# GpSimd's order of work inside an attention slot, in a fused cross-attention and coupled feed-forward kernel

## The reference

```
xn  = layernorm(x)                                   # no weights: (x - mean) / sqrt(var + eps)
u   = heads(xn) . heads(ctx) * scale / 4             # 16 heads of 16
a   = softmax(where(mask, -inf, tanh(u) * exp(log_C)))
x   = x + (a . heads(ctx)) @ W_out.T
f   = layernorm(x);  gf = global_net(mean of f over the tokens)
for 3 cycles:
    tf = coupling_net(f)         # 256 -> 256 -> 128 -> 64 -> 1, gelu between, sigmoid at the end
    f  = f + (0.1 + range * (0.7*gf + 0.3*tf - 0.5) * 2) * twist(f)
x   = x + f
```

## Time and profile before

| what | value |
|---|---|
| median of three runs | 1072.22 us (1072.2 to 1073.6) |
| the profiled execution's own time | 1072.12 us |
| its span in the profile | 1070.2 us |
| mean granted TensorE clock | 0.983 of full |
| busy: PE, ACT, DVE, POOL | 977.3, 901.5, 843.8, 573.9 us (91%, 84%, 79%, 54%) |

### The profile page before, as it was taken

The page is one execution under the profiler, slowest core; times in us unless marked ns, Lnnn a source line. Parts: engine busy times, 40 slices in busy tenths (PEclk is TensorE's granted clock), DMA queues, the critical chain, the costliest instruction groups (busy, mean ns, idle before and its releaser), DMA issues.

```text
span 1070.2 us, 21910 instructions
## 1 busy us (share of the span) xinstructions
PE 977.3 (91%) x7260; PEld 526.2 (49%) x7260; DVE 843.8 (79%) x1770; ACT 901.5 (84%) x1121; POOL 573.9 (54%) x1053
## 2 busy tenths in 40 slices
PE   6899999999899999999999999999989999996993
PEld 4456435554355544555445543555435554454431
DVE  3888796997879886987869879699796988688485
ACT  3999778997799978998789977899779997895575
POOL 3366604876068740887228870487606874087204
PEclk7999999999999999999999999999999999999897
DMA  5433002430033200432005310153002430020002
GB/s 118 88 59 58 6 2 44 103 88 1 1 75 89 71 1 1 98 89 48 1 1 118 88 30 1 36 112 88 0 2 69 92 74 1 2 54 31 11 1 80
DMA packets 191119, 51.71 MB, mean 48 GB/s; under 512 B 165920, under 2 KB 174624, under 8 KB 191008
## 3 DMA queue, kind: packets, MB, share of 16 engines
q1 hardware_dynamic: 191008, 50.31, 22.2%
HBM read 33.37 MB, written 16.78 MB: 47 GB/s over the span
## 4 chain that ended last, share of the span: by engine, by line
PE 43%; DVE 16%; POOL 14%; ACT 13%; issue 10%; SPq 2%; DMA 1%; DVEq 0%; POOLq 0%; ACTq 0%
PE ps L1255 8%; PE ps L1269 7%; PE ps L1239 6%; PE ps L1159 5%; ACT probs L914 5%; PE ps L1190 4%; ACT probs L920 3%; PE ps L1175 3%; POOL f_hat L470 3%; PE ps L1278 2%; POOL twisted L525 2%; DVE move_u L780 2%; DVE move_u L801 2%; DVE move_v L782 2%; POOL q_hat L449 2%
## 5 line engine op out<-in xcount | busy, mean ns | idle before, releaser
L914 ACT ACTIVATE probs<-ps,u_scale 120x2048 f32<-120x2048 f32 x128 | 253.7, 1982 | 23.2 <-PE ps L1159 23.2
L920 ACT ACTIVATE probs<-probs,exp_bias,clip 120x2048 f32<-120x2048 f32 x128 | 270.2, 2111 | 0.1
L1269 PE MATMUL ps<-h,w 128*128 128x512 f32 x384 | 185.5, 605 | 14.5 <-ACT h L948 13.8
L1159 PE MATMUL ps<-q_t,k_t 32*120 32x256 f32 x2048 | 148.9, 405 | 21.5 <-ACT probs L914 20.6
L489 POOL TENSOR_TENSOR c<-tok_c 128x16 f32<-128x16 f32 x8 | 1.8, 223 | 277.8 <-issue 277.8
L1190 PE MATMUL ps<-wo_t,of_t 128*128 128x256 f32 x512 | 143.5, 403 | 1.0 <-DVE xy L717 1.0
L692 DVE STREAM_TRANSPOSE o_t<-ps 128x512 f32<-128x512 f32 x128 | 90.6, 708 | 68.0 <-PE ps L1175 67.7
L1175 PE MATMUL ps<-probs,va 120*32 120x256 f32 x2048 | 138.7, 389 | 1.6 <-ACT probs L920 1.5
L1159 PEld LDWEIGHTS ps<-q_t,k_t 32*120 32x120 f32 x2048 | 93.4, 180 | 58.7 <-issue 51.4
L1269 PEld LDWEIGHTS ps<-h,w 128*128 128x128 f32 x384 | 67.5, 189 | 93.0 <-issue 66.0
L1190 PEld LDWEIGHTS ps<-wo_t,of_t 128*128 128x128 f32 x512 | 86.9, 189 | 49.9 <-issue 41.7
(11 more groups left out here) (132 smaller groups left out, 1791.5 us busy)
## 6 DMA issues: line engine op xcount, KB each, us to landing
xy<-in_x_dram SPq DMA_DIRECT2D x64, 256.0 KB, 3.3
out_dram<-xy SPq DMA_DIRECT2D x64, 256.0 KB, 2.1
cbuf<-in_ctx_dram SPq DMA_DIRECT2D x64, 120.0 KB, 2.8
va<-in_ctx_dram SPq DMA_DIRECT2D x64, 120.0 KB, 3.6
tok_c<-coup SPq DMA_DIRECT2D x256, 0.5 KB, 2.0
move_v<-in_L_xattn_W_out_dram SPq DMA_DIRECT2D x1, 256.0 KB, 5.2
move_u<-in_L_ffn_cn_w_dram SPq DMA_DIRECT2D x1, 256.0 KB, 3.3
w<-in_L_ffn_cn_w_dram SPq DMA_DIRECT2D x1, 128.0 KB, 3.1
```

Of the source, the lines that this page charges most:

```text
L914: eng.activation(probs[:, b % 2, n * HALF:(n + 1) * HALF, :].rearrange("k h q -> k (h q)"), banks(SCORE_BANK, 4)[0:KEYS, :], ACT.Tanh, sca ...
L920: eng.activation(p, p, ACT.Exp, scale=clip[0:KEYS, 0:1], bias=exp_bias[:, b:b + 1]).then_inc(s_exp, 1)
L1159: last = eng.matmul(banks(SCORE_BANK + r)[0:KEYS, odd * S:(odd + 1) * S], k_t[rows, b % 2, odd, n, :], q_t[rows, b % 2, n, :], start=True, ...
L1269: last = eng.matmul(banks(bank), w2[:, k, :], h1[:, p % 2, k, :], start=(k == 0), stop=(k == EK - 1))
```

## The change

In each slot the order on POOL becomes: `norm_2_scale`, `norm_2`, then (place 4 only) a low half, `query_scale` and `query_hat` back to back, then the coefficients where there are any, the old batch's two parts, and last a low half in places 2, 4 and 7. Before, the order was `norm_2_scale`, `query_scale`, `norm_2`, coefficients, the two parts of the old batch, `query_hat`, and a low half in places 2, 3, 5 and 6. No instruction is added, removed or resized, and no other engine's program changes.

```diff
-        LOW_AT = (2, 3, 5, 6)
+        LOW_FIRST = {4: (0, 1)}
+        LOW_LAST = {2: (0, 0), 4: (1, 0), 7: (1, 1)}
...
                 if 0 <= i - LAG < NB:
                     norm_2_scale(i - LAG)
+                    norm_2(i - LAG)
+                if place(i) in LOW_FIRST:
+                    low_half((i - LAG) // GROUP, *LOW_FIRST[place(i)])
                 if new is not None and 2 <= new < NB:
                     query_scale(new)
-                if 0 <= i - LAG < NB:
-                    norm_2(i - LAG)
+                    query_hat(new)
                 if after_ffn(i):
                     coefficients(groups_before(i) - 1)
                 for b in late[:2] if after_ffn(i) else late[:1]:
                     twisted_part(b)
                     x_part(b)
                 late = late[2:] if after_ffn(i) else late[1:]
-                if new is not None and 2 <= new < NB:
-                    query_hat(new)
-                if place(i) in LOW_AT:
-                    part = LOW_AT.index(place(i))
-                    low_half((i - LAG) // GROUP, part // EK, part % EK)
+                if place(i) in LOW_LAST:
+                    low_half((i - LAG) // GROUP, *LOW_LAST[place(i)])
```

## The result

The changed kernel takes 1066.28 us (median of 4 runs, 1065.68 to 1067.46), the kernel before 1072.47 beside it (4 runs, 1072.2 to 1073.6): a ratio of 0.9942, 95% interval 0.9924 to 0.9959. Forecast were 1065.5 us and 1063.0 to 1069.8. The profiled execution took 1066.2 us, with a span of 1064.3 (before: 1072.12 and 1070.2).

The account below looks back on a forecast made before the run. ACT was taken to pace the attention phases, held by late POOL work, and POOL to bound the last phase's end. 3.26 + 1.4 + 1.5 + 0.5 = 6.6 us off 1072.12 gave 1065.5 us, 8-in-10 range 1063.0 to 1069.8.

Parts of the forecast that it names:

- The mechanism: Attention phases: ACT sets the pace, and its gaps come from PE's scores, made late by POOL's `f_hat` and `q_hat`.
- The gaps: ACT, phases 1 to 6: all 17 gaps before the tanh over the scores close, a gain of 3.26 us.
- just ahead of each gap PE waits for POOL: PE, phase 1: waits of 0.30 us for `f_hat`, 0.86 and 0.63 us for `q_hat` were read as preceding ACT's gaps.
- The start of the feed-forward: PE at a phase's end: last full slot's tanh to L1255 falls to phase 0's 6.74 us, 1.4 us gained.
- The low halves in the middle: POOL, places 3 to 7: moving the low halves costs nothing, with 1 us of cover before the feed-forward.
- The old batch's parts behind `q_hat`: POOL, places 3 and 4: DVE's combine still finds them ready, tightest margin 0.5 us or so; costed at nothing.
- The last phase: End of the last phase: last `f_hat` and PE's work come 1.5 us earlier, plus 0.5 us from the clock.
- The step for the clock: PE after its last-phase wait: a quarter of the 2.1 us lost at half clock comes back, 0.5 us.
- The clock fell: Rival, last phase: the clock holds at full, 2.1 instead of 0.5 us gained, 1063.9 us; chance 0.15.
- Nothing else held the scores: Rival, attention phases: something else holds the scores; 1070.6 us if all the middle is held, 1068.3 if half; chance 0.15.
- Collisions: Rival, DVE's places 5 and 7: more collisions with POOL, about 1081 us, or 1073.7 with one more a slot; chance 0.08.
- The half in place 7: Rival, feed-forward: this low half comes too late if it slips by 1 us, each further one costing 7 us; chance 0.02.

Follow-up runs that it names:

- the two single moves: On the kernel before: `query_hat` alone moved ahead of the old batch, 1070.87 us; `norm_2` alone moved ahead of `query_scale`, 1071.37 us.
- the queries alone: Kernel before with only `query_hat` moved ahead of the old batch's two parts: 1070.87 us, ratio 0.998.
- four buffers: Four coupling buffers instead of two: on the changed kernel 1063.88 us, on the kernel before 1070.25 us.
- the two reorders alone: Changed kernel with both moves in the order, but the low halves left in places 2, 3, 5 and 6: 1067.29 us, ratio 0.9941.
- two kernels with a shorter wait: Changed kernel with the last old batch's parts behind the last `norm_2`: 1063.18 us; the same with four coupling buffers: 1062.18 us.

## Why the prediction was right, point by point

*The mechanism held, but for one gap's source.* The gaps on ACT were POOL's lateness, all closed, and nothing took their place: PE waits for ACT's own tanh inside the phases. That both reorders were needed was implied by costing them together and is shown by the two single moves. One reading was wrong: "just ahead of each gap PE waits for POOL". The wait for `q_hat` at 230.30 comes behind the third gap (228.74) and stands in phase 1 alone, where it held up L1255. Phases 2 to 5 have two waits for POOL (`f_hat`, `q_hat`) for their three gaps, and phase 6 one for its two: the last gap goes with the `q_hat` before it.

*The gaps were sized too small: 3.26 us forecast, 5.8 by spacing.* I summed the idle times that the trace prints. The cost of a gap is the spacing of the starts: 202.90 - 198.03 = 4.87 us before against 202.98 - 198.43 = 4.55 after, so 0.32 where 0.16 was printed. For the other two it is 0.39 against 0.24, and 0.28 against 0.16: 0.99 us for phase 1 against a printed 0.56. Two ACT instructions in a row overlap, and the printed length shows it: 1.97 us behind a gap, 2.02 to 2.09 in the rows of after. A gap loses this overlap as well, and one below the smallest that the trace prints still costs 0.30, as the queries alone showed. By spacing, phases 2 to 5 come to 1.0 each like phase 1, and phase 6 to 0.7. From the first tanh of a phase to the last slot's, which takes in every start between, it is 51.34 to 51.38 us before (51.04 in phase 6) and 50.30 or 50.31 after: 6.0 us.

*The start of the feed-forward was too large: 1.4 us forecast, about nothing net.* I took phase 0's 6.74 us from the row of the chain of waits, whose 101.83 is not the start of the instruction: in ACT's timeline it starts at 101.57, which makes 7.00. Against that, phases 2 to 6 (6.90) had nothing to win, only phase 1 had: 7.32 before, 235.11 - 228.13 = 6.98 after. With 0.3 won there and some 0.08 of each other phase going the other way by this measure (6.90 before, 6.98 after), nothing is left. The two errors cancelled in part: 3.26 + 1.4 = 4.7 forecast against 5.8 in this pair of profiles. Odd feed-forwards do not explain the rest: from the first L1255 to the next phase's first tanh the six stretches sum to 413.96 us before and 414.12 after. With four buffers in both kernels the same count gives 5.0, because the slots of the kernel before take 51.23 to 51.25 us in phases 1 to 5 there, not 51.34 to 51.38: its second gap is smaller (0.17 to 0.19 printed, 0.24 to 0.27 before in phases 1 to 5). Why is open.

*The low halves in the middle cost nothing:* right for the changed kernel (the two reorders alone have the same middle), though with little to spare. The one in place 7 takes 1.59 us and not 1.16, and in phase 1 ends at 237.11, 0.95 us ahead of PE's first L1239; on the kernel before, the moved low halves cost 1.4 us in one group of a profile. In the last phase they are the gain: right.

*The old batch's parts behind `q_hat`:* right. DVE's combine has no wait for them in places 3 and 4 of phase 1.

*The last phase was too large: 1.5 + 0.5 = 2.0 us forecast, 1.16 - 0.66 = 0.5 measured.* The chain came 1.16 us earlier, not 1.5, and PE's last wait is 3.90 us, forecast near 3.5. POOL's timeline of the changed kernel, against the earlier trace rows:

```profile
977.12 0.32 POOL L458 TENSOR_SCALAR var<-mv 128x2 f32<-128x2 f32 x1 [0.91 <-DVE mv L730]
...
980.79 1.09 POOL L535 TENSOR_SCALAR xy<-xy,x_fac,x_add 128x256 f32<-128x256 f32 x2
981.97 0.46 POOL L458 TENSOR_SCALAR var<-mv 128x2 f32<-128x2 f32 x1
```

The wait for DVE's statistics took the low half's place, as forecast. Counted from the first L1255 of the phase, place 6's norm starts 0.22 us earlier (982.74 - 872.23 before, 977.12 - 866.83 after; forecast 0.39). From there to place 7's norm, which now follows on the old batch's L535 with no low half between, it is 4.85 us, 5.96 before: 1.11 less, as forecast. From that norm to the last L1203 it is 984.78 - 981.97 = 2.81, 2.64 before: 0.17 more, with the norm's first instruction at 0.46 instead of 0.28 us. The step for the clock had the wrong sign: I let it return a quarter of its loss, and it lost 0.66 us more. I bounded the loss by what the kernel before showed, 2.1 us, and not by the work that could run at half if the fall came later. The loss goes by when the fall comes: 3.6 us ahead of the work the twelve products took 3.94 us (four buffers), 2.5 ahead 4.45 (before), 1.1 ahead 5.16 (after). In the five profiles with a last wait of 3.9 us and nothing put into it, what follows the first of these products takes 77.48 to 78.61 us, and in the four with one of 4.8 to 4.9 us 77.57 to 77.95, so the sign of this term is that of one pair of profiles and not of the change. The Trainium skill (TensorE: Matmul & The Clock Gate, Part 1, The HAM clock gate) ties the lower clock to an idle TensorE and the higher to a busy one; the kernel with fourteen unread products agrees, at 1.00 and 2.75 us for the twelve L1255 instead of 0.50 and 5.16.

*The rivals.* The clock fell in the changed kernel too; it held with unread products and in one of two kernels with a shorter wait. Nothing else held the scores. Collisions moved from DVE to POOL: DVE's busy time fell from 843.8 to 839.3 us, POOL's grew by 11.3. The groups by line of the changed kernel (busy us, mean ns):

```profile
L471 POOL TENSOR_SCALAR f_hat<-xy,neg,rstd 128x256 f32<-128x256 f32 x128 | 98.5, 776 | 13.6 <-POOL rstd L461 13.6
...
L704 DVE TENSOR_TENSOR o_n<-o_t,inv_sum 128x512 f32<-128x512 f32 x64 | 47.9, 749 | 7.0 <-DVE inv_sum L700 0.5
...
L814 DVE TENSOR_TENSOR xy<-xy,twisted 128x256 f32<-128x256 f32 x56 | 25.2, 450 | 2.0 <-POOL xy L535 2.0
```

`f_hat` was 644 ns in the mean before, DVE's two were 795 and 489: POOL, which now has room, pays, and DVE gains. DVE's only wait for POOL's parts of the old batch is in the last phase, 2.05 us (2.35 before). The half in place 7 was never late in the changed kernel; with a second one ahead of it, it was, and cost 1.0 us.

Of the sum, then, 6.6 us forecast (the terms make 6.66) and 5.9 measured, the middle was 1.1 too small and the last phase 1.5 too large, with 0.4 of the rest in the first stretch. That stretch ends anywhere between 108.46 and 110.06 us in these profiles, whatever the kernel. The closeness of the total is partly luck.

## What to carry to other kernels

Price a stall on the bounding engine by the spacing of its instructions' starts against an undisturbed stretch, not by the printed idle time, and take starts from the engine's timeline, not from a chain that cuts them. When two late tensors come from one in-order engine, expect a single reorder to win little while the other tensor is still late. Ahead of a stretch that only TensorE sets, look for what makes it wait: the wait is paid once more if the clock falls shortly before the work comes back.

## What the runs showed of the hardware that was not expected

- The granted clock fell in one profile and not in another with the same waits on PE in the same place, twice: 1.67 and 1.63 us at the end of the last phase, and 0.42, 1.20 and 0.58 us in a feed-forward (phases of 128.30 and 126.68 us). Six unread products in each of the last two waits, 1.46 us of work, kept it at full and were worth 1062.18 - 1059.80 = 2.4 us. What tips it otherwise stays open.
- Single transfers of 0.5 KB rows held a buffer 0.3 to 1.7 us beyond the moment when ACT wanted it, one to five times in each profile looked at with two buffers. Four buffers removed it, and with it ACT's waits for DVE's L801: together 1.0 us off the changed kernel's phases 1 to 6, and 1.3 off the median of the kernel before.
- Where POOL's and DVE's instructions met in the places shown, the one that began later lost most: POOL's two over 128x256 took 3.27 us instead of 1.1 behind DVE's `move_u`; DVE's took 1.52 and 1.65 instead of 0.69 behind POOL's low halves. A start 0.06 us ahead was enough, and what it set off cost 1.4 us.
